# First 128 rows of scores as one full-precision product per head, ahead of the other rows, in an attention and mixture-of-experts layer

## The reference

```
h = layernorm(x) * (1 + ca) + sa
q, k, v = h W_Q, h W_K, h W_V                  # 16 heads of 64
scores = q k^T / 8, causal mask, softmax
x = x + ga * (probs v W_out + b_out)
h = layernorm(x) * (1 + cb) + sb
weights = softmax over the 2 best of 8 experts of h Wr + br
x = x + gb * sum_e weights_e * (gelu(h W1_e + b1_e) W2_e + b2_e)
```

## Time and profile before

| | |
|---|---|
| Median of three runs | 1893.16 us |
| Runs | 1892.86 to 1893.52 us |
| The profiled execution's own time | 1894.34 us |
| Its span, first to last instruction | 1892.5 us |
| TensorE busy | 1871.9 us (99%) |
| VectorE busy | 1663.3 us (88%) |
| ScalarE busy | 1534.0 us (81%) |
| GpSimd busy | 729.3 us (39%) |
| Mean granted TensorE clock | 0.999 |

### The profile page before, as it was taken

How to read it: one execution, slowest core, us unless ns; L and a number is a source line. 1 busy time by engine, 2 the same in 40 slices (tenths; PEclk the granted TensorE clock), 3 DMA queues, 4 the chain that set the end, 5 groups by cost and what they waited for, 6 DMA issues and landing times.

```text
span 1892.5 us, 50829 instructions
## 1 busy us (share of the span) xinstructions
PE 1871.9 (99%) x15450; PEld 1429.8 (76%) x15450; DVE 1663.3 (88%) x4388; ACT 1534.0 (81%) x3664; POOL 729.3 (39%) x1212
## 2 busy tenths in 40 slices
PE   8999999999999999999999999999999999999999
PEld 6777777777777777777777777888888888888887
DVE  7888898898898898888898898989899889989998
ACT  6888888888888888888888988877777777777775
POOL 3445445445445445445445452222222222222221
PEclk9999999999999999999999999999999999999999
DMA  4200000000000000000000002111111111111111
GB/s 121 69 2 1 1 0 1 1 0 1 1 0 1 1 0 1 1 0 1 1 0 1 1 2 90 46 56 50 50 50 50 50 50 50 50 50 50 51 54 53
DMA packets 42622, 50.04 MB, mean 26 GB/s; under 512 B 3160, under 2 KB 24464, under 8 KB 42512
## 3 DMA queue, kind: packets, MB, share of 16 engines
q1 hardware_dynamic: 42256, 48.41, 8.0%
q0 software_dynamic: 256, 0.53, 0.1%
HBM read 44.47 MB, written 4.46 MB: 26 GB/s over the span
## 4 chain that ended last, share of the span: by engine, by line
PE 81%; ACT 8%; issue 6%; DVE 3%; POOL 0%; DVEq 0%; ACTq 0%; DMA 0%; POOLq 0%
PE banks L603 11%; PE banks L576 9%; PE banks L590 7%; PE banks L682 6%; PE banks L683 6%; PE banks L684 6%; PE banks L701 6%; PE banks L703 6%; PE banks L702 6%; ACT probs L948 5%; PE banks L523 4%; PE banks L525 3%; PE banks L524 3%; DVE probs_T L1225 2%; PE banks L625 1%
## 5 line engine op out<-in xcount | busy, mean ns | idle before, releaser
L501 POOL TENSOR_SCALAR probs<-probs,rdenom 128x512 f32<-128x512 f32 (+3 forms) x1024 | 523.5, 533 | 598.1 <-DVE rdenom L1241 598.1
L948 ACT ACTIVATE probs<-probs,neg_max 128x512 f32<-128x512 f32 (+3 forms) x1024 | 564.2, 553 | 87.5 <-DVE neg_max L1232 86.8
L1053 ACT ACTIVATE hidden<-banks,b_cols 128x512 f32<-128x512 f32 x512 | 349.6, 688 | 177.7 <-PE banks L684 177.3
L1411 DVE TENSOR_TENSOR hid_lo<-hidden,hid_hi 128x512 fp32r<-128x512 f32 x512 | 380.3, 754 | 56.8 <-ACT hid_hi L1061 41.9
L1232 DVE CUSTOM_DVE_ANT_0 probs<-banks,mask_w 128x512 f32<-128x512 f32 (+3 forms) x1024 | 427.9, 483 | 1.4 <-PE banks L576 0.6
L487 POOL TENSOR_TENSOR acc<-acc,y_w 128x512 f32<-128x512 f32 x110 | 151.4, 1376 | 462.7 <-DVE y_w L1424 461.0
L603 PE MATMUL banks<-probs_T,v_sb 128*64 128x512 f32 (+3 forms) x2048 | 303.9, 439 | 0.3 <-issue 0.3
L603 PEld LDWEIGHTS banks<-probs_T,v_sb 128*64 128x64 f32 x2048 | 136.6, 136 | 154.8 <-issue 117.6
L1225 DVE COPY probs_T<-banks 128x512 f32<-128x512 f32 (+1 forms) x256 | 235.8, 950 | 13.4 <-PE banks L590 11.1
L682 PE MATMUL banks<-h_hi,w_hi 128*128 128x512 f32 x512 | 205.8, 402 | 0.1
L590 PEld LDWEIGHTS banks<-ident,probs 64*128 64x128 f32 x5120 | 174.4, 140 | 37.5 <-issue 35.2
(11 more groups left out here) (180 smaller groups left out, 3393.2 us busy)
## 6 DMA issues: line engine op xcount, KB each, us to landing
w_rows<-w_kept SPq DMA_DIRECT2D x128, 256.0 KB, 4.5
x_all<-in_L_attn_resid_dram SPq DMA_DIRECT2D x16, 256.0 KB, 2.8
w_raw<-in_L_ffn_W_dram SPq DMA_DIRECT2D x16, 256.0 KB, 4.9
out_dram<-y_result SPq DMA_DIRECT2D x15, 256.0 KB, 2.3
v_sb<-in_L_attn_W_V_dram SPq DMA_DIRECT2D x1, 512.0 KB, 8.1
hidden<-in_L_attn_W_out_dram POOLq DMA_DIRECT2D x2, 256.0 KB, 7.5
v_sb<-in_L_attn_W_Q_dram SPq DMA_DIRECT2D x1, 448.0 KB, 5.2
v_sb<-in_L_attn_W_K_dram SPq DMA_DIRECT2D x1, 448.0 KB, 6.0
```

The lines of the kernel that those rows point to most:

```text
L501: pool.tensor_scalar(part, part, rdenom[:, p % 2, 4 * h + r:4 * h + r + 1], 1.0, ALU.mult, ALU.mult)\
L948: act.activation(part, part, ACT.Exp, bias=neg_max[:, p % 2, col:col + 1], scale=-1.0, accum_out=denom[:, p % 2, col:col + 1]).then_inc(p_ ...
L1053: act.activation(hidden[:, e % 2, c, :], banks[:, c, :], ACT.Gelu, bias=b1_cols[:, e * HC + c:e * HC + c + 1]).then_inc(hid, 1)
L1411: dve.tensor_tensor(hid_lo[:, e % 2, c, :], full, hi.bitcast(F32), ALU.subtract)\
```

## The change

For row tile 0, GpSimd adds the parts of the first 128 columns of q and of k back together (`join`, into the new `q_full` and `k_full`, two halves each), after it has scaled the probabilities of the pair two before. TensorE multiplies them in full precision, one product per head (`first_rows`), and does this before unit 0 of the scores; `scores` leaves out row tile 0. `first_rows` writes banks 4 and 5, so it has the waits of unit 1 (`t_dve`), and the waits for `x_mid` and `h_full` now stand in front of it. On ScalarE the last exponential of head 1 moves in front of `h_evac`, `round_h` and `half_out`.

```
+            q_full = sa("q_full", [P, 2, P])
+            k_full = sa("k_full", [P, 2, P])
...
                                         .then_inc(p_norm, 1)
+                            if not (last and p >= NP - 2):
+                                join(*after(*after(b, p)))
+
+                    def join(b, p):
+
+                        wait_alone(pool, q_lo, pair(1, b, p) + 1)
+                        pool.tensor_tensor(q_full[:, p % 2, :], q_hi2[:, p % 2, 0:P].bitcast(F32),
+                                           q_lo2[:, p % 2, 0:P].bitcast(F32), ALU.add).then_inc(q_whole, 1)
+                        wait_alone(pool, k_lo, pair(1, b, p) + 1)
+                        pool.tensor_tensor(k_full[:, p % 2, :], k_hi2[:, p % 2, 0:P].bitcast(F32),
+                                           k_lo2[:, p % 2, 0:P].bitcast(F32), ALU.add).then_inc(k_whole, 1)
+
+                    join(0, 0)
+                    join(0, 1)
                     batches(pool, body)
...
+                    def first_rows(b, p, begin, young):
+                        pe.wait_ge(q_whole, pair(1, b, p) + 1)
+                        pe.wait_ge(k_whole, pair(1, b, p) + 1)
+                        if young and not begin:
+                            pe.wait_ge(s_masked, 6)
+                        if not young:
+                            pe.wait_ge(t_dve, pair(2, b, p) - 3)
+                        at = ROW_IN_BANK[0]
+                        for h in range(2):
+                            own = slice(h * DH, (h + 1) * DH)
+                            pe.matmul(S_BANK[1][h][:, at:at + P], q_full[own, p % 2, :], k_full[own, p % 2, :],
+                                      start=True, stop=True)
...
                         for r in UNITS[u]:
+                            if r == 0:
+                                continue
...
-                            scores(b, p, 0, begin, young)
                             if p == 5 and not first:
                                 pe.wait_ge(x_mid, b)
                             if p == 6 and not last:
                                 pe.wait_ge(h_full, b + 2)
                             if p == 6 and last:
                                 pe.wait_ge(r_full, 1)
+                            first_rows(b, p, begin, young)
+                            scores(b, p, 0, begin, young)
                             scores(b, p, 1, begin, young)
...
                         for n, i in zip(put[1:], now[1:]):
                             values_out(b, n, i)
+                        exponentials(b, p, 1, 2)
                         if p == 5 and not last:
...
-                        exponentials(b, p, 1, 2)
                         if not begin:
                             evac_T(*prev, first and p == 1)
```

More of the change, by code:

```diff
@@ L356, in adaln_moe_kernel @@
             q_lo = sem("q_lo")
+            q_whole, k_whole = sem("q_whole"), sem("k_whole")
             k_lo = sem("k_lo")
```

## The result

The changed kernel takes 1936.35 us (median of four runs, 1935.98 to 1937.09) against 1893.22 us for the kernel before in the same comparison: a ratio of 1.0228, 95% interval 1.0215 to 1.0241. It is 43 us slower. The forecast was 1933 us.

A forecast was written before the change was run, and what follows sets the result against it. TensorE bounds the attention stage, two engines close behind. Changed steps sum to +2.49 us a batch, times 15.5 batches 38.6, plus about 1 at the start: +39.6, median 1933 us (own range 1918 to 1950; range 1908 to 1960).

The forecast's parts named there:

- The cover of unit 0: Attention scores: the copy freeing banks 4 and 5 ends late, hidden by unit 0's 0.79 us; the change removes that cover.
- F: Start of TensorE's first product of a pair's scores; steps from one to the next total some 71 us a batch.
- The loop: Four engines: mask F + 1.41, first exponential F + 2.14, `k_hi` F + 6.48, D F + 7.70; 8.47 us a pair.
- D: Start of VectorE's copy of transposes unit 2, which frees banks 4 and 5; the copy takes 0.68 us.
- The start of a pair, D + 0.77: TensorE's earliest F: copy ends D + 0.68, k joined D + 0.70, plus some 0.07 us for the semaphore.
- The moved waits of p = 4 and 5: Next F waits for `x_mid` (step 9.05 us for 8.23, +0.82) and for `h_full` (9.60 for 8.51, +1.09).
- the old hole: TensorE's p = 6 gap before unit 1, caused by ScalarE's `h` read-out; its removal gives 9.98 us for 10.78, −0.80.
- The exponentials: ScalarE: the exponential moved ahead of `h_evac` fits into 0.67 us of idle time; sooner exponentials are worth nothing by themselves.
- The price of the product: TensorE row tile 0: 0.27 us for 0.28, gaining 0.01 us a pair, at best 0.06, 8 us over 128 pairs.
- The number of batches: Attention stage: first and last batch lack some waits, so 15.5 batches at +2.49 us each are counted, 38.6 us.
- swallowed by slack: Rival, 10%: VectorE and ScalarE catch up during stalls, only the p = 5 and 6 terms stay, about 1911 us.
- the two heads' products do overlap: Against a 7% rival: TensorE's full-precision heads run one after the other, 28 us more, 1961 us.

## Why the prediction was right, step by step

**The cover of unit 0.** Right. The copy of banks 4 and 5 ends behind F in five of eight pairs, which cost nothing as long as 0.79 us of work for other banks stood in front. The run with the waits alone gives 36 us of the 43.

**The loop.** Right that four engines wait for each other in a circle, and that this is longer than TensorE's own 7.96. F + 1.41, F + 2.14, F + 6.48 and F + 7.70 were forecast. Measured were F + 1.34, 2.07 and 6.43, and D at F + 7.62 in p = 1 and 7. Each forecast was 0.05 to 0.08 too late: 0.03 because the product ahead of unit 0 costs 0.24 (457.45 to 457.69) and not 0.27, and as much again because F + 1.1 and 0.27 make 1.37 and not 1.41. The rows of the kernel before have D at F + 7.58 already, so the product in front lengthens this part by 0.04 us where the sum had 0.12. Most of what makes the loop longer is the step from D to the next F.

**The start of a pair, D + 0.77.** Right for the copy (F − D is 0.73 in p = 3), too small for the join: 0.92 in p = 0 and 2. The term that was mis-sized is the way from GpSimd to TensorE. The addition takes 0.46 as taken, and starts 0.15 behind `k_lo`. But from its end (456.76 + 0.46 = 457.22) to F it is another 0.24 us, where 0.07 was put. The loop's 7.62 for 7.70 takes back half of it: it is 8.55 and not 8.47. That the errors have opposite signs is luck.

**The moved waits of p = 4 and 5.** Right: 9.09 and 9.54 for 9.05 and 9.60. For p = 4 this is again two errors that cancel, 7.62 for 7.70 and F at D + 1.47 for D + 1.35. The experiment that leaves them out takes 19 us off, where 17 were expected. For p = 2 0.38 was forecast and 0.27 measured. In p = 6 the old hole is gone, −0.86 for −0.80.

**The exponentials.** Right as far as it was tried: they fit into idle time and give nothing, alone or with the product at its old place.

**The price of the product.** The forecast of 8 us at best from the product alone was near: 6 us at the old place, from 0.10 us a pair and not 0.06. Only four pairs keep it: with the product at its old place the steps of p = 1, 4, 6 and 7 are 0.11 to 0.13 us shorter, that of p = 2 by 0.04, and those of p = 0, 3 and 5 not at all.

**The number of batches.** The sum had 2.49 us a batch, 15.5 times, and 1 us at the start: 39.6. The 14 whole batches in the middle are 2.41 each (70.96 to 73.37), 33.7 together. But up to the second pair of batch 2 the change had already lost 4.4 us (94.87 to 99.25), and from the second pair of the last batch to the end 4.7, with 42.8 in all. The two ends cost 9.1 where 4.7 was counted. The sum was near because 2.49 a batch was a little too much and the ends were too little.

At the start two things add to the first batch's own longer steps. TensorE's first product waits for the joins: it follows the end of the first `k_lo` by 2.00 us (14.82 to 16.82) where it took 0.46 before (15.66 to 16.12), so the joins cost 1.5 there and not 1. The second pair then waits for the masks of the first, because `first_rows` moves that wait too; the kernel with the fast products in front, which has no joins, stands just as long. The first product of the second pair, in the change and in that kernel:

```profile
23.05 0.80 PE L583 MATMUL banks<-k_full,q_full 64*128 64x128 f32 x4 [2.56 <-DVE neg_max L1264]
21.28 0.33 PE L581 MATMUL banks<-k_hi,q_hi 64*128 64x128 f32 x2 [2.57 <-DVE neg_max L1262]
```

The first step is 6.22 us in the change, 6.35 with the fast products in front, 5.29 before and 5.29 with the waits alone, where the masks' wait isn't moved. At the end it is the last pair above all. Its copy starts 0.78 us behind F in the kernel before (1140.49 against 1139.70), and TensorE stood 0.56 us ahead of unit 1 even then; now it stands 2.19 us ahead of the pair, and the step before it takes 9.97 us for 8.23. In this pair the granted clock fell as well. TensorE before, TensorE after, and stretches of the changed kernel (the columns are those of the earlier trace rows, the third number from the end is the granted clock):

```profile
1141.22 0.44 PE L576 MATMUL banks<-k_hi,q_hi 64*128 64x384 f32 x2 [0.56 <-DVE probs_T L1225]
1182.03 0.46 PE L583 MATMUL banks<-k_full,q_full 64*128 64x128 f32 x3 [2.19 <-DVE probs_T L1257]
1180.00:1182.00 2.00, 0.00 (x0) 0.00 (x1) 1.41 (x3) 1.47 (x3) 0.38 (x1) 1.00 0.00 0
1182.00:1184.00 2.00, 1.97 (x18) 1.99 (x20) 1.74 (x5) 0.00 (x0) 0.71 (x2) 0.77 0.00 0
1184.00:1186.00 2.00, 2.00 (x12) 1.07 (x11) 2.00 (x13) 1.89 (x5) 2.00 (x5) 0.50 0.00 0
1186.00:1188.00 2.00, 2.00 (x15) 0.80 (x11) 0.76 (x6) 1.22 (x6) 1.39 (x4) 0.88 0.00 0
```

0.50 is the lower of TensorE's two levels, 1.2 GHz; in the same pair of the kernel before the clock stayed at 1.00. How the 9.1 us divide among these causes is read from the timelines, and no run tests it apart.

The rivals: little of the loss was swallowed by slack (the 0.17 us of ScalarE's waiting time in the loop), and the two heads' products do overlap (four instructions in 0.24 us). The Trainium skill (FP8 and Floating Point Precision, TensorE Precision Notes) counts four passes for true FP32. The trace agrees: two instructions of 0.11 us each for 128 columns. As four passes against three it would have made the product a loss, and it is a gain, because the fast products of this width cost more than their columns.

## What to carry to other kernels

A wait belongs behind the work that needs nothing from it. Before an instruction is moved up in an engine's list, look at what its waits were hidden by, and read how late the releaser ends against the new place; where it ends later, the move costs that, and once more whatever the other engines then start later, less the time for which they waited anyway. A cheaper form of a product is to be tried first where the old one stood: here that alone gives 6 us, and the same product in front costs 43.

## What the runs showed of the hardware

- Two full-precision products, one per head (64 rows, 128 columns), inside a run of products take 0.14 us until the next one starts (502.14 to 502.28), and with what follows 0.10 less than six fast ones of that width. As first of a stretch they take 0.24 against 0.39.
- TensorE goes on 0.06 us after a copy of VectorE ends (p = 3 of the change, p = 0 and 2 with the waits alone), but 0.24 us after GpSimd's addition ends (p = 0 and 2 of the change, four pairs with the longer join). In the sequence of waits the copy's comes behind the join's, so a part of the 0.24 may be the waits' own processing, and the ends of GpSimd's instructions are rough in the profile; neither was tried apart.
- GpSimd adds 128x128 float32 in 0.46 us and 128x512 in 1.29 (78 of the 110 in the expert stage; the other 32 start beside an instruction of VectorE, see below, take up to 1.7 and lift the mean to 1.38). The Trainium skill (GPSIMD Engine Reference, Elementwise — side-by-side cycle accounting) gives 2.6 cycles per element, an estimated 0.28 us for 128 columns. The trace agrees: 384 more columns take 0.83 us more, which is 0.28 per 128. An estimated 0.18 us are left as the fixed part.
- An addition on GpSimd that starts while VectorE works on an instruction with two inputs from the on-chip memory, and none from the banks, is held up until that has ended. In the six kernels with joins there are 38 such additions, beside `wk_lo`, `wo_lo` and `h_lo`; every one of them ends 0.31 or 0.32 us after VectorE's instruction, whenever it started. All others take 0.45 to 0.47 us, also those that were under way when such an instruction began, and those beside `k_lo`, one of whose inputs lies in the banks. The first addition of the changed kernel is one of the 38, which is a part of the late start; in the kernel with the joins alone it starts 0.86 us after `wk_lo` has ended and takes 0.46. VectorE and GpSimd in the change, the first addition with the joins alone, and one beside `h_lo` in that kernel:

```profile
14.86 1.09 DVE L1317 TENSOR_TENSOR wk_lo<-v_sb,wk_hi 128x896 fp32r<-128x896 f32 x1
15.21 1.06 POOL L513 TENSOR_TENSOR q_full<-q_hi,q_lo 128x128 f32<-128x128 f32 x1 [5.28 <-DMA wr_sb<-in_L_ffn_Wr_dram]
...
16.73 0.46 POOL L513 TENSOR_TENSOR q_full<-q_hi,q_lo 128x128 f32<-128x128 f32 x1 [7.01 <-DMA wr_sb<-in_L_ffn_Wr_dram]
...
218.17 0.69 DVE L1239 TENSOR_TENSOR h_lo<-hf,h_hi 128x512 fp32r<-128x512 f32 x1
218.28 0.90 POOL L516 TENSOR_TENSOR k_full<-k_hi,k_lo 128x128 f32<-128x128 f32 x1
```
